# Expert loop: inverse roots as powers on GpSimd, weighting on ScalarE, four output buffers, scatters three tiles behind; with changes of the head and of the routing

## The reference

```
# L0_attn_ref(layernorm(x)), channel by channel
q = 1 - sigmoid(delta) * sigmoid(alpha)
k = einsum('dnl,dn->dl', sigmoid(delta) * beta * exp(arange(l) * log(q)), gamma * sqrt(1/16))
x = x + causal_convolution(layernorm(x), k) + layernorm(x) * omega
# L0_ffn_ref(layernorm(x)): the output has 4096 tokens' worth of rows added
order = argsort(expert_indices.reshape(-1), stable=True); tok = order // 2
for e in range(8):
    h  = gelu(xr @ w1A[e].T @ w1B[e], approximate=False)
    ye = h @ w2A[e].T @ w2B[e]
    out = out + (bin_ids == e)[:, None] * ye
y = zeros.at[tok].add(flat_w[order][:, None] * out)
x = x + y
```

## Time and profile before

| | us |
|---|---|
| median of 3 runs | 1204.19 |
| lowest, highest | 1199.62, 1209.06 |
| the profiled execution | 1210.82 |
| its span, first to last instruction | 1208.9 |

### The profile page before, as it was taken

How to read it: one execution, slowest core, us unless ns; L and a number is a source line. 1 busy time by engine, 2 the same in 40 slices (tenths; PEclk the granted TensorE clock), 3 DMA queues, 4 the chain that set the end, 5 groups by cost and what they waited for, 6 DMA issues and landing times. The chain is left out here.

```text
span 1208.9 us, 34118 instructions
## 1 busy us (share of the span) xinstructions
PE 926.7 (77%) x11452; PEld 748.2 (62%) x11452; DVE 874.9 (72%) x1495; ACT 843.8 (70%) x1191; POOL 621.3 (51%) x755
## 2 busy tenths in 40 slices
PE   4740488849858668999999999988988898485980
PEld 2530477747747556777777777776767777374770
DVE  6976897958869346778777787776548888496880
ACT  4852598959959645767667676766768989495970
POOL 4132686848755225666666666675663333232320
PEclk9985799989979979999999999998999989798995
DMA  7999695999999798999988888986349599999909
GB/s 235 337 400 325 180 214 155 278 276 293 255 287 336 208 309 240 253 266 252 253 228 218 231 211 220 238 216 136 98 114 222 109 288 261 281 274 271 279 4 274
DMA packets 337536, 287.89 MB, mean 238 GB/s; under 512 B 18088, under 2 KB 285000, under 8 KB 336962
## 3 DMA queue, kind: packets, MB, share of 16 engines
q1 hardware_dynamic: 292866, 211.22, 64.0%
q0 software_dynamic: 19520, 36.26, 15.1%
q10 hardware_dynamic: 25088, 39.60, 10.0%
HBM read 197.41 MB, written 100.61 MB: 247 GB/s over the span
## 5 line engine op out<-in xcount | busy, mean ns | idle before, releaser
L1335 PE MATMUL ps<-xn,wb 128*128 128x128 f32 x2048 | 276.3, 291 | 0.0
L509 POOL TENSOR_TENSOR cen<-xb,mean 128x512 f32<-128x512 f32 x128 | 143.2, 1119 | 250.7 <-DVE state L1163 158.2
L1335 PEld LDWEIGHTS ps<-xn,wb 128*128 128x128 f32 x2048 | 251.4, 200 | 17.2 <-issue 2.7
L939 ACT ACTIVATE cen<-ps 128x1024 f32<-128x1024 f32 x156 | 156.0, 1022 | 138.3 <-PE ps L1429 119.8
L1322 PE MATMUL ps<-xn,near 128*32 128x128 f32 x2048 | 85.8, 286 | 166.1 <-DVE xn L1136 118.5
L1136 DVE TENSOR_TENSOR xn<-cen,rstd 128x1024 f32<-128x1024 f32 x128 | 176.5, 1379 | 49.2 <-POOL cen L509 41.1
L1429 PE MATMUL ps<-carry,wb 64*128 64x256 f32 x1248 | 170.8, 404 | 27.7 <-DVE carry L1210 27.1
L1322 PEld LDWEIGHTS ps<-xn,near 128*32 128x32 f32 x2048 | 51.8, 112 | 189.2 <-issue 89.2
L1442 PE MATMUL ps<-cen,xn 128*64 128x128 f32 x2496 | 161.4, 277 | 0.9 <-ACT cen L939 0.8
L1442 PEld LDWEIGHTS ps<-cen,xn 128*64 128x64 f32 x2496 | 136.8, 137 | 38.3 <-issue 22.8
L1147 DVE TENSOR_TENSOR xb<-xb,ps 128x1024 f32 (+1 forms) x128 | 152.9, 1194 | 8.6 <-PE ps L1347 8.6
(11 more groups left out here) (164 smaller groups left out, 1349.8 us busy)
## 6 DMA issues: line engine op xcount, KB each, us to landing
out<-xb SPq DMA_DIRECT2D x116, 512.0 KB, 6.7
xb<-L_attn_x SPq DMA_DIRECT2D x96, 512.0 KB
xb<-L_attn_x SPq DMA_DIRECT2D x32, 1024.0 KB, 10.9
xb<-L_attn_x ACTq DMA_DIRECT2D x128, 256.0 KB
wb<-L_ffn_w_B SPq DMA_DIRECT2D x78, 256.0 KB
wide<-taps_d SPq DMA_DIRECT2D x60, 256.0 KB
y_d<-xb SPq DMA_DIRECT2D x16, 512.0 KB
dk<-decay_d SPq DMA_DIRECT2D x60, 128.0 KB
```

Source lines behind the costliest of these rows:

```text
L509: pool.tensor_tensor(cen[:, k, 0:QB // 2].rearrange("p b r d -> p r b d"), unit_view(pool, g, i, k)[:, :, 0:UC // 2] .rearrange("p r (b d) ...
L939: act.activation(act_h[:, b % 2].rearrange("p f t -> p (f t)"), ps[:, 2 * (b % 2):2 * (b % 2) + 2, :].rearrange("p a t -> p (a t)"), ACT.G ...
L1335: ins = pe.matmul(ps[:, QB * k + b, d * P:(d + 1) * P], wb[:, h, k * QB + b, d, :], xn[:, k, 2 * b + d, :], start=(b > 0 and d == 0), stop ...
```

## The change

What it does, part by part:

- **Roots.** The tokens' inverse deviation is no longer sqrt on ScalarE and reciprocal on DVE, but an add of EPS and a `pow` with exponent -0.5 on POOL (`deviation`); for the second half's rows too (`deviations2`). ScalarE's dummy GELUs between tiles go.
- **Weighting.** `weigh` moves from DVE to ScalarE (a Copy with a scale per partition), between the second and the third GELU. Only the last tile's stays on DVE.
- **Output buffers and order on POOL.** Four buffers per half tile, two in `carry` and two in the new `lag`; scatters come three tiles behind instead of one and are caught up in tiles NQ-4 to NQ-1. The gather is for three tiles ahead and stands behind `stage_down` 1 instead of at the start.
- **Loop.** The body has four tiles instead of two; 5 tiles ahead of it and 6 behind it stand alone. The second half's statistics are two instructions per tile in the last tiles.
- **DVE.** `rank_in_half` has three copies instead of four: the second pair of halves is laid down crosswise, and `down` takes the other side.
- **Head.** Loads of x go first on SP; the four parameter loads move to ScalarE's queue; three memsets go behind the fourth copy; `row_stats` of two loads goes ahead of the tables' start; 36 of the routing's instructions move to POOL, three behind each copy from the ninth on (sums over experts as trees of adds); of four blocks of taps and decays two are loaded by SP behind the last x load. The head's slot scatters follow later copies.
- **Around the loop.** In the first half's last column tile three `copy_out` instead of two, and the first half of the columns of y's four pieces, are stored early; `up_load` and w2B wait for the gathers.
- **Last store.** Half of the last column tile's columns is stored once its first 8 units are done, in 256 B rows; the other half at the end.

The diff, cut to its core ("..." where lines are left out):

```diff
...
+        root = sb("root", [P, 2])
+        lag = sb("lag", [P, 2, 2 * D])
...
-            with eng.Fori(2, TT // 2 + 1) as p:
-                tile(p * 2 - 1, 1, False, True)
-                tile(p * 2, 0, False, True)
...
+            for q in range(5):
+                tile(q, q, q == 0, q > 0)
+            with eng.Fori(0, TT // 4 - 1) as p:
+                for j in range(4):
+                    tile(p * 4 + (5 + j), (5 + j) % 4, False, True)
+            for q in range(TT + 1, NQ):
+                tile(q, q % 4, False, False)
+        def route_o(m, h):
+            return out_lag[:, m - 1, h, :] if m in (1, 2) else out_near[:, m // 3, h, :]
...
@@ POOL, head
-            const(pool.memset(wb[:, 0, :, :, 0:2 * ZR], 0.0))
-            const(pool.memset(near[:], 0.0))
+            const(pool.memset(root[:], -0.5))
-            const(pool.memset(shift_s[:], 0.0))
...
             for n in range(NL):
                 keep(n)
-                if NL // 2 <= n < NL // 2 + SENT:
-                    send(n - NL // 2)
+                if n == LBUF - 1:
+                    pool.memset(wb[:, 0, :, :, 0:2 * ZR], 0.0).then_inc(s_late, 1)
+                    pool.memset(near[:], 0.0).then_inc(s_late, 1)
+                    pool.memset(shift_s[:], 0.0).then_inc(s_late, 1)
+                if n >= 2 * LBUF:
+                    for _ in range(3):
+                        next(rest, None)
+                if n >= NL - SENT - 1 and n < NL - 1:
+                    send(n - (NL - SENT - 1))
...
@@ POOL, expert loop
+            def deviation(q, k):
+                hold(pool, s_tv, 2 * q + 2, s_const)
+                pool.tensor_scalar(tstd[:, k, :], tmean[:, k, :, 1], EPS, None, ALU.add).then_inc(s_tw, 1)
+                hold(pool, s_tw, q + 1, s_const)
+                pool.tensor_tensor(trstd[:, k, :], tstd[:, k, :], root[:], ALU.pow).then_inc(s_ts, 1)
+            def deviations2():
+                r = rstd[:, P:2 * P]
+                pool.wait_ge(s_dv, 2 * DV_STATS - 1)
+                pool.tensor_scalar(r, var[:, P:2 * P], EPS, None, ALU.add).then_inc(s_std, 1)
+                pool.wait_ge(s_std, 2)
+                pool.tensor_tensor(r, r, root[:, 0:1].to_broadcast([P, P]), ALU.pow).then_inc(s_dv, 1)
+            def scatters(q, m):
+                if not isinstance(q, int):
+                    scatter(q - 3, (m + 1) % 4)
+                    return
...
+                ready = {NQ - 4: (q - 3, q - 2), NQ - 3: (q - 2,), NQ - 2: (q - 2, q - 1), NQ - 1: (q - 1,)}
+                for p in ready.get(q, (q - 3,) if q >= 3 else ()):
+                    scatter(p, p % 4)
-            def tile(q, k, first, rows):
-                if is_in(q, NQ - 2):
-                    gather(q + 2, k)
-                if is_in(q, NQ - 1):
+            def tile(q, m, first, rows):
+                if first:
+                    gather(2, 0)
+                if more:
                     e = expert(pool, q + 1)
                     stage_up(q + 1, e)
                     stage_down(q + 1, e, 0)
...
+                scatters(q, m)
+                if more:
+                    stage_down(q + 1, e, 1)
+                if is_in(q, NQ - 3):
+                    gather(q + 3, 1 - k)
+                if more:
+                    stage_down(q + 1, e, 2)
+                if is_in(q, NQ - 2):
+                    deviation(q + 2, k)
+                if more:
+                    stage_down(q + 1, e, 3)
+                if isinstance(q, int) and q == NQ - 2:
+                    deviations2()
...
@@ SP
+            for k in range(LBUF):
+                sp.dma_start(loadbuf[:, k], x_rows[:, k * LR:(k + 1) * LR, :]).then_inc(s_load[k], 16)
...
+                    if final and g == 1 and b == BT - 1:
+                        store_early(g, t, range(PIECES))
+            def store_early(g, t, pieces):
+                sp.wait_ge(s_ev, UT * t + UT // 2)
+                for j in pieces:
+                    store_part(g, t, j, slice(0, P // 2), s_early)
...
+            for h in range(2):
+                sp.wait_ge(s_g[h], 16)
             up_load(0, 0)
-            up_load(1, 1)
+            for h in range(2, 4):
+                sp.wait_ge(s_g[h], 16)
...
-            store_tile(1, NT - 1, range(PIECES))
+            for j in range(PIECES):
+                store_part(1, NT - 1, j, slice(P // 2, P), s_put[j])
...
@@ ScalarE, expert loop
+            def weigh(q, m, h):
...
+                wait(act, s_s[2 * k + h], 8 * (q - (2 + k)))
+                wait(act, s_wo, 2 * (q + 1))
+                act.activation(route_o(m, h), ps[:, 6 + h, :], ACT.Copy, scale=slot_w[:, bass.ds(col, 1)])\
...
                 for b in range(4):
+                    if b == 2 and not first:
+                        for h in range(2):
+                            weigh(q - 1, (m + 3) % 4, h)
...
-                if is_in(q, NQ - 2):
-                    deviation(q + 2, k)
-                    gelu_table()
...
@@ DVE, expert loop
-                if h == 0:
-                    wait(dve, s_ts, q + 1)
-                    dve.reciprocal(trstd[:, k, :], tstd[:, k, :]).then_inc(s_ch, 1)
...
             def rank_in_half(q):
                 wait(dve, s_a, q + 1)
+                dve.tensor_copy(route_a[:, 0, :], ps[:, 5, 0:P]).then_inc(s_at, 1)
                 for h in range(2):
-                    for m in range(2):
...
+                    dve.tensor_copy(route_a[(1 - h) * RANK:(2 - h) * RANK, 1, :],
+                                    ps[h * RANK:(h + 1) * RANK, 5, 0:P]).then_inc(s_at, 1)
...
-                if not first:
-                    for h in range(2):
-                        weigh(q - 1, 1 - k, h)
-                    stage_out(q)
                 if is_in(q, NQ - 2):
                     token_stats(q + 2, k)
+                if not first:
+                    stage_out(q)
...
```

More of the change, by code:

```diff
@@ L590, in _ @@
             stage_up(0, e)
+            deviation(0, 0)
+            deviation(1, 1)
             over_tiles(pool, tile)
@@ L658, in _ @@
             sp.wait_ge(s_keep, NL)
+            for k in range(TB):
+                sp.wait_ge(s_tapd[k], 16 * (NK // TB))
+            sp.wait_ge(s_dec, 16 * NK)
+            sp.wait_ge(s_tab, 16)
             def load_weights(i, k):
@@ L819, in _ @@
             act.wait_ge(s_dec, 16 * NK)
-            for k in range(WB):
+            for k in range(2):
                 row = taps_d[k:k + 1].rearrange("k s i d -> k (s i d)")
@@ L838, in steps @@
                     wait(act, s_pe, QB * (u - 1))
-                    if first and k == 1 and i == NK:
-                        for j in range(2):
-                            act.wait_ge(s_s[j], 16 * ((NQ + 1) // 2))
                     act.activation(carry[:, k, 0:CR + P], far[:], ACT.Exp, scale=rate[:, bass.ds(col, 1)])\
@@ L965, in _, with row_stats @@
             stats1 = wb_row[:, KC * ER:KC * ER + 6 * P].rearrange("p (r f) -> p r f", f=6)
-            def row_stats(q):
-                for k in range(LBUF):
+            def row_stats(q, bufs=range(LBUF)):
+                for k in bufs:
                     wait(dve, s_load[k], 16 * (q + 1))
@@ L1111, in _ @@
             next(parts)
-            row_stats(0)
-            next(parts)
+            row_stats(0, (2, 3))
             row_stats(1)
@@ L1116, in _ @@
             row_stats_rest()
-            statistics(0, stats1)
+            for _ in statistics(0, stats1):
+                pass
+            dve.wait_ge(s_std, 1)
+            dve.reciprocal(rstd[:, 0:P], rstd[:, 0:P]).then_inc(s_dv, 1)
+            dve.wait_ge(s_dv, DV_STATS)
             def centre(g, i, k):
@@ L1229, in stage_out, with tile @@
                 dve.tensor_copy(w2bs, w2bd[:, bass.ds(col, D)]).then_inc(s_w3, 1)
-            def tile(q, k, first, rows):
+            spread = statistics(1, stats2)
+            def tile(q, m, first, rows):
+                k = m % 2
                 if not first:
@@ L1256, in tile @@
                     keep2(q, LR2 // 2)
+                else:
+                    if q == TT + 1:
+                        dve.wait_ge(s_free2, P // 2)
+                    if q > 0:
+                        next(spread, None)
+                        next(spread, None)
             token_stats(0, 0)
+            token_stats(1, 1)
             for h in range(2):
                 normal(0, 0, h)
-            token_stats(1, 1)
             rank_in_half(0)
-            def spread():
-                dve.wait_ge(s_free2, P // 2)
-                statistics(1, stats2)
-            over_tiles(dve, tile, spread)
+            over_tiles(dve, tile)
             rank_out(NQ - 1)
```

227 lines of the change are left out of this document (123 added, 104 removed).

## The result

The changed kernel takes 1219.1 us, the one before 1204.4 (medians of five runs each on the same chip): the ratio is 1.0121, with a 95% interval of 1.0081 to 1.0161. The forecast was 1152, so it was wrong in sign: the kernel was to be 52 us faster and is 15 us slower. The profiled execution of the changed kernel has a span of 1219.8 us, against 1208.9.

A forecast was written before the change was run, and what follows sets the result against it. The prediction took PE, held up by late gathers through DVE, with POOL nearly as full, to bound the loop. Terms 14 + 4 + 22 + 2 + 10 = 52 us off the 1204.2 us median gave 1152, range 1126 to 1184.

The forecast's parts named there:

- The head: Stage before the first half: four terms, sum 17.3 us, less 3 us allowance, so -14 us; bounds 9 and 17.
- terms 1 and 2: Head: loads of x issued first, 3.6 us; fifth load sent at about 11 instead of 20.60, 4.8 us.
- Term 3: Head: all but one of 25 routing instructions between loads 12 and 13 leave DVE, 4.8 us.
- term 4: Head: two of four blocks of taps and decays go behind the last load, 4.1 us.
- Into the loop: Between first half and expert loop: large loads wait for the gathers, first statistics start sooner; -4 us, bounds 1 and 7.
- The loop: Expert loop: gathers issued one tile earlier end the waits, POOL's 11.2 us cycle sets the pace; -22 us, bounds 0 and 36.
- rival (b): Loop: POOL's addition reaches 1.4 us per tile, so the loop gains nothing; 1174 us, chance 0.14.
- Rival (a): Loop: PE's 10.76 us floor holds because POOL hides the power; loop -36, total 1138 us, chance 0.18.
- Rival (c): Loop: the four-tile body is fetched anew each of seven rounds, 7 to 21 us; 1166 us, chance 0.12.
- Out of the loop: Loop exit: ScalarE's 4.96 us wait for `carry` goes, about half showing at PE; -2 us, bounds -4 and +6.
- The last store: Last stage: half the columns stored early, remaining half takes 18.9 instead of 29.2 us; -10 us, bounds 0 and 11.
- Rival (d): Last store: 256 B writes are dear, 57 ns per packet; 1223 us, decides from 49 ns on, chance 0.04.

The follow-up runs named there:

- statlate: Changed kernel with DVE's statistics of the first two loads again behind the routing's first part; 1222.7 us (one run).
- parfirst: Changed kernel with the four parameter transfers again on SP ahead of the loads of x, instead of on ScalarE's queue; 1223.6 us, ratio 1.0138.
- twice: Changed kernel with each tile's 128x2 power on POOL computed twice; 1243.9 us, ratio 1.0335.
- tileroot2: Changed kernel with the tiles' inverse roots again a square root on ScalarE and a reciprocal on DVE, the 128x128 power kept; 1203.4 us, ratio 0.9976.
- spread: Changed kernel with the pairs of scatters at tiles 37 and 38 instead of 35 and 37; 1212.3 us, ratio 1.0083.
- best: Changed kernel with no power on POOL (all roots on ScalarE and DVE) and the scatter pairs at tiles 37 and 38; 1179.1 us, ratio 0.9796.
- root2: Changed kernel with the second half's 128x128 power on POOL again a square root on ScalarE and a reciprocal on DVE; 1199.3 us, ratio 0.9951.
- whole: Changed kernel with the last column tile stored in one piece at the end, in 512 B packets; 1229.2 us, ratio 1.0181.
- tailonly: Kernel before the change with only the early store of half the last column tile's columns added; 1196.8 us, ratio 0.9917.
- late: Kernel best with scatters 35 and 36 in tile 38, and 37 and 38 behind the second half's first two centrings; 1180.2 us, ratio 0.9789.

## Why the prediction was wrong, step by step

**The head: right in kind, -8.5 instead of -14.** The fifth copy came 5.3 us sooner, of the 8.4 that terms 1 and 2 together gave, but at the ninth 2.7 were left. Term 3 (routing off DVE) gave 3.3 of 4.8 (lead at the 13th copy 6.1, at the ninth 2.7), and term 4 (two blocks of taps) 2.6 of 4.1: the two that stay still make a gap of 4.19 us. The allowance of 3 us was too small. What failed is the way of adding: I took four gaps as if each could be shortened by itself, while statlate (7.9 us at the fifth load, 2.4 at the last) and parfirst (4.8 us on DVE's first instruction, nothing at the end) show that a delay put in or taken away at one place of the head is in part made up at the next. Where it goes between the fifth and the ninth load can be read from DVE's statistics of the loads, in the kernel before and in the changed one:

```profile
17.94 9.59 DVE L974 BATCH_NORM_STATS2 wb<-xb 128x6 f32<-128x512 f32 x16
...
12.69 4.83 DVE L1093 BATCH_NORM_STATS2 wb<-xb 128x6 f32<-128x512 f32 x8
...
22.81 11.96 DVE L1093 BATCH_NORM_STATS2 wb<-xb 128x6 f32<-128x512 f32 x20
```

The statistics of loads three and four start at 22.7 before (half of the 16 instructions from 17.94 on) and at 22.81 after: DVE starts 4.7 us later, since the parameters do, and has no gap of more than 0.2 us between 12.69 and 34.8. So only the buffers of loads one and two come free clearly sooner. I had put the late parameters on the table chain alone, with 10 us of cover, and overlooked that DVE's first statistics stand behind them: SP issues the fifth load at 15.33, not at my 11. The result lies just outside my bounds of 9 and 17.

**Into the loop: about right.** `widen(0)` is 14.05 us sooner, 8.5 of it from the head, so 5.5 against my 4. One reading in it was skewed: of the two times I set against each other, the 10.4 us count from the first gather of a tile and the 3.7 from the second (713.22; the first of that tile was issued at 711.82).

**The loop: -22 forecast, +13.5 came.** Four steps failed.

- POOL's cycle: 11.71 measured, 11.2 forecast. The term "power and add 0.8 us" was mis-sized: from the add's start to that of the next copy it is 1.07 (609.52 to 610.59). The other 0.2 of the 1.27 us lie between the two scatters of this cycle (2.15 us from start to start, 1.95 before); the five weight copies cost the same as before. With 1.27 us the loop's steady part was where rival (b) had put it, at no gain. Rival (b) named 1.4 as the point, since the tile that had to be beaten was mis-sized too: my 11.85 us are a mean over the loop with its first two tiles (28.2 us) and the three around the block of statistics (41.6); between them, from the fourth to the 31st `widen`, it was 11.61. There the mean tile is now 11.76 us, and my 11.2 was 15 us short over these 27 tiles. twice and tileroot2 show that POOL's cycle sets it: +0.87 on POOL makes +0.71 per tile, and without the pair the tile falls from 11.66 to 11.27 where both were measured. The gather did cease to be the bound, as forecast, but what took its place was as long.
- The pair at tile 35: the tile takes 22.8 us, 12 over PE's 10.8, forecast 4 for both pairs. I had named what stands behind it (gather, power, two copies), and put about 4 us for the scatter and no figure for its wait, which is 4.94. In spread, without the pair, the tile is 11.3 us shorter.
- The first three tiles: 40.7 us, against 33.6. The first takes 18.97: PE waits 6.42 us at 451.94 in `up` of tile 2, for no releaser that the trace names. SP issued that tile's weights at 438.38, behind five pieces of stores with 3.5 MB. Its two transfers landed 11.0 and 12.8 us after they were issued, the last of them at about 452, when PE goes on; the median of these loads is 5.1. No run takes the stores away, so the cause is read from this trace and not tested. The kernel before lost as much over its first two tiles (28.2 us, 30.0 now).
- Tiles 31 to 34 took 48.5 us where my pace gives 44. The block of statistics in front of tile 33 did go: before, three tiles of 13.0, 15.0 and 13.6; now one of 14.4.

PE's wait of the third point:

```profile
451.94 3.79 PE L1529 MATMUL ps<-carry,wb 64*128 64x256 f32 x16 [6.42 <-issue]
```

Rival (a), PE's floor, was far off. Rival (c), fetches of the longer body: instruction queues moved 9 pieces between 480 and 830 (3 before), and the tile times show no period of four. best has the same body and moves 15 pieces between 480 and 840, and about half of its tiles there take 10.8 us, PE's floor. Nothing speaks for it, though no run isolated it.

**Out of the loop: -2 forecast, +22 came.** This is the step that turned the sign. The power of 128x128 was bounded by "0.3 us to some 8 us" and taken at the low end, "by the small rows"; it took 20.77, two and a half times the upper bound, and undoing it alone (root2) gives 20 us back. ScalarE's wait of 4.96 us for `carry` did go, and shows nowhere: root2, without the power, still starts the second half 3.7 us later after its last `widen` than the kernel before. 2.68 of these are scatter 37's wait for the pair in tile 37, by its trace; the rest was not looked into.

**The last store: right.** 10 us forecast, whole and tailonly give 10 and 8.5. In the changed kernel between 1200 and 1218, DMA packets and the queue's share:

```profile
DMA packets 15416, 3.89 MB, mean 216 GB/s; under 512 B 15415, under 2 KB 15415, under 8 KB 15415
...
q1 hardware_dynamic: 15415, 3.89, 97.5%
```

That is 18 us x 16 / 15416 = 18.7 ns for a packet of 256 B, against the 18.4 taken, and 28.5 for one of 512 B. Rival (d) needed 49. The Trainium skill's "DMA: Bandwidth & Descriptors", Specifications, gives 512 B as the least size for the full rate and says that the engine reads, modifies and writes below it. The trace agrees on the rate (216 against 283 GB/s) and does not show what the engine does; with it a half still takes two thirds of the time of the whole.

The sum by the measured terms: -8.5 - 5.5 + 13.5 + 22 - 10.5 = +11, as the spans show.

## What to carry to other kernels

An operation that no row shows must be bounded from above per element, not per instruction: one instruction at a place where everything queues behind it decides a change, and its size would have put 20 us in the range: the forecast's own 0.8 us for two elements, taken per element, is 51 us for 128. Add up an engine's whole cycle before work is moved onto it, and where it is the pace-maker count every tenth of a microsecond, since it is paid in each tile; work moved away from engines that only wait is worth nothing. Work that is put off (scatters three tiles behind) is a debt, and its second instalment waits for the first to land: look at what stands behind it in the queue at the end of the loop, for putting it off once more (late) only moved the wait.

## What was not expected of the hardware

- POOL's power: 0.4 us plus 0.16 us per element of each partition, from 2 to 128 elements. The full operand (128x2) and the broadcast ones (128x8 and wider) lie on one line. With two elements it costs 0.72 us, three times an add of the same shape (0.23).
- POOL's copy of 128x256 took 0.40 us at some places and 0.59 at others with the same shape, both in the same tile. What makes the difference was not isolated.
- A scatter that adds to `out` takes 5.1 to 5.3 us from issue to landing in the changed kernel, 7.0 to 7.6 in best and late (medians), so a second one that must keep its order made POOL stand still: 4.94 us at tile 35, 3.45 in late, but only 1.29 at tile 37.
